# Expert weights in 16 planes, slot rows by one gather, scores and v transposes by halves among the output projection, initial loads in another order

## What is computed

```python
xn = layernorm(x)
q = xn @ Wq + bq                          # 1024 -> 16 heads of 64
k, v = split((xn @ Wdown + bdown) @ Wup + bup)   # through a latent of 256
q, k = rope(q), rope(k)
att = softmax(einsum('thd,tgd->thg', q, k) / 8)  # over the 16 heads g of ONE token
out = einsum('thg,tgd->thd', att, v) @ Wout + bout
logits = xn @ router_w.T + router_b       # 8 experts
y = (xn @ expert_w[top1].T + expert_b[top1]) * max(softmax(logits))
result = x + out + y
```

## Time and profile before

| | us |
|---|---|
| median of three runs | 1162.58 |
| lowest, highest | 1150.81, 1163.72 |
| profiled execution, whole | 1148.63 |
| its span on the slowest core (core 2) | 1147.0 |
| spans of the other cores | 1114.9 to 1141.8 |
| mean granted TensorE clock of core 2 | 0.811 |

### The profile page before, as it was taken

One profiled execution on the slowest core, in us unless ns is written; L12 is line 12 of the kernel. 1 busy time (PEld: TensorE's weight loads), 2 busy tenths in 40 slices (PEclk: granted clock), 3 DMA queues, 4 the chain that ended last, 5 costly groups with the idle time before them and its releaser, 6 DMA issues.

```text
span 1147.0 us, 26610 instructions; the slowest of 8 cores (1114.9 to 1147.0 us)
## 1 busy us (share of the span) xinstructions
PE 768.5 (67%) x10170; PEld 441.5 (38%) x10170; DVE 403.6 (35%) x864; ACT 295.9 (26%) x424; POOL 152.6 (13%) x151
## 2 busy tenths in 40 slices
PE   0626566775857664767866867746362899899984
PEld 0514253544535352545535535433221333333331
DVE  2414434343534443344544534535220121221211
ACT  0313232323241431325234243231220111111110
POOL 2000000000000000000000000001101334344331
PEclk9957676766779686877878878777766999999998
DMA  9966293938577593924335245261932476777785
GB/s 187 191 156 46 95 112 102 151 54 147 41 154 56 158 72 124 142 72 121 78 110 129 38 139 126 52 121 51 189 66 83 93 129 124 135 125 126 129 120 71
DMA packets 73353, 126.64 MB, mean 110 GB/s; under 512 B 12874, under 2 KB 42571, under 8 KB 73236
## 3 DMA queue, kind: packets, MB, share of 16 engines
q0 software_dynamic: 21936, 53.27, 36.5%
q1 hardware_dynamic: 51300, 71.67, 23.8%
HBM read 88.99 MB, written 45.91 MB: 118 GB/s over the span
## 4 chain that ended last, share of the span: by engine, by line
PE 46%; issue 17%; DMA 12%; DVE 9%; SPq 5%; DVEq 5%; ACT 3%; another core or an unknown queue 1%; POOL 0%; ACTq 0%; POOLq 0%
PE ps L1006 17%; PE ps L863 7%; PE ps L814 7%; DMA ks<-ks 6%; PE ps L837 5%; SPq L1022 4%; DMA vs<-vs 4%; DVEq L497 3%; PE ps L948 2%; ACT vs L712 2%; DVE pe L500 2%; DVE stats L399 2%; PE ps L982 2%; PE ps L934 1%; PE ps L902 1%
## 5 line engine op out<-in xcount | busy, mean ns | idle before, releaser
L1006 PE MATMUL ps<-wexp,xgT 128*128 x624 | 200.4, 383 | 22.1 <-issue 20.7
L814 PE MATMUL ps<-wo_sb,oT 128*128 128x512 bf16 x512 | 150.8, 448 | 0.0
L302 POOL DMA_INDIRECT tab<-meta,sloti x32 | 31.5, 985 | 722.9 <-DVEq L471 718.0
L863 PE MATMUL ps<-xnT,wq_sb 128*128 128x256 bf16 x1024 | 121.7, 283 | 0.0
L632 DVE TENSOR_SCALAR y<-ps,metab 128x1024 f32<-128x1024 f32 x39 | 50.1, 1284 | 201.0 <-PE ps L1006 201.0
L1006 PEld LDWEIGHTS ps<-wexp,xgT 128*128 128x128 bf16 x624 | 60.2, 96 | 157.0 <-issue 155.9
L863 PEld LDWEIGHTS ps<-xnT,wq_sb 128*128 128x128 bf16 x1024 | 102.6, 101 | 17.1 <-issue 1.2
L742 ACT COPY xgT<-ps 128x1024 bf16<-128x1024 bf16 x39 | 39.5, 1012 | 227.6 <-PE ps L982 227.6
L837 PE MATMUL ps<-xnT,wdn_sb 128*128 128x256 bf16 x256 | 53.3, 397 | 59.7 <-DVE x1b L512 21.0
L814 PEld LDWEIGHTS ps<-wo_sb,oT 128*128 128x128 bf16 x512 | 57.6, 112 | 80.6 <-issue 47.6
L483 DVE TENSOR_REDUCE mx<-ps 128x16 f32<-128x512 f32 x32 | 21.9, 686 | 165.0 <-PE ps L934 165.0
(11 more groups left out here) (139 smaller groups left out, 823.1 us busy)
## 6 DMA issues: line engine op xcount, KB each, us to landing
xT_sb<-xT SPq DMA_DIRECT2D x16, 1024.0 KB, 8.0
wexp<-exw POOLq DMA_DIRECT2D x16, 1024.0 KB, 22.3
xs<-xn SPq DMA_DIRECT2D x16, 512.0 KB, 9.6
x0b<-x SPq DMA_DIRECT2D x4, 1024.0 KB, 8.2
x1b<-x SPq DMA_DIRECT2D x4, 1024.0 KB
x2b<-x SPq DMA_DIRECT2D x4, 1024.0 KB, 12.2
qs<-qs SPq DMA_DIRECT2D x32, 128.0 KB
ks<-ks SPq DMA_DIRECT2D x32, 128.0 KB
```

Of the source, the lines that this page charges most:

```text
L814: ins = mm(out=ob, lhsT=oT[h][:, 128 * k:128 * k + 128], rhs=wo[:, 1024 * k + 512 * n:1024 * k + 512 * n + 512], start=False, stop=(k == 7))
L863: ins = mm(out=ps[:, 512 * b + 256 * c:512 * b + 256 * c + 256], lhsT=wq[:, 1024 * k + 128 * m:1024 * k + 128 * m + 128], rhs=xnT[:, 256 * ...
L1006: ins = mm(out=bank(2 + 2 * (j % 3) + n), lhsT=xgT[j % 2][:, 128 * k:128 * k + 128], rhs=wexp[:, bass.ds(wof, 8192)] [:, 1024 * k + 512 * ...
```

## The change

**Weights.** The experts' weights become 16 tensors ("planes") `wx[c]`, c = 8n + k, each with one column block of 512 of all eight experts. A matmul's address is the register (512 times the expert) plus its plane's start. Four registers are loaded at a time, once in four tiles. The lower half of each plane (experts 0 to 3, `elo`) is loaded in blocks 1 to 8, two a block, now behind the scatters of the same block; buffers of the first part lie in the upper halves, which are loaded by `ehi` from block 14 on. All weights and the transposed x come from the host in an order in which each partition reads one contiguous piece.

**Table.** `tile_table` moves to block 15 and gives a row number for each tile; one gather brings the 39 rows of 128 slots, and DVE and PE turn them into columns (`meta_rows`, two transposes, `meta_cols`). The first two expert tiles run before the last block's attention and output projection.

**Blocks on PE.** Scores and v transposes run half by half (h outermost), each half in two parts, and parts of the output projection stand between them; its first group stands ahead of `av` of half 1. The banks of the projection and of the latent change. **On DVE** the statistics move a block ahead (those of x(i+2) in block i), `routing2(i)` moves from the end of block i-1 to behind block i's first q evacuation, the projection's evacuations move ahead of `sm2`. **On SP** `xsstore(i+1)` goes first in the loop. **At the start** the first weights are issued before the iotas, `wq` in four pieces with a semaphore each, the five small loads go to ACT's queue.

```diff
+    wx = [at("wx%d" % c, [128, 4096], BF16, EXP0 + 8192 * c) for c in range(16)]
...
+            wload(wdn[:], wdn_d, d_wdn)
+            wload(wq[0][:], wq_d[0], d_wq[0])
             iota(icol[:], [[0, 1]], cm=1)
...
+            def elo(c):
+                wload(wx[c][:, 0:2048], exw_d[c][:, 0:2048], d_elo)
+
+            def ehi(c):
+                wload(wx[c][:, 2048:4096], exw_d[c][:, 2048:4096], d_ehi)
...
-            scatter(0)
             for i in range(NT):
+                scatter(i)
                 if 1 <= i <= 8:
-                    eload((i - 1) // 2, (i - 1) % 2)
-                if i == 14:
+                    elo(2 * i - 2)
+                    elo(2 * i - 1)
+                if i == NT - 2:
                     gpsimd.wait_ge(d_o[0], 32 * 4)
+                    ehi(0)
+                    ehi(1)
                     gpsimd.wait_ge(p_rp, NT)
-                    for half in range(2):
-                        eload(4, half)
-                if i + 1 < NT:
-                    scatter(i + 1)
+                    ehi(2)
+                    ehi(3)
+            gpsimd.wait_ge(p_q, 4 * NT)
+            for c in range(4, 8):
+                ehi(c)
+            gpsimd.wait_ge(p_v, 2 * NT)
+            gpsimd.wait_ge(d_xs, 16 * NT)
+            for c in range(8, 13):
+                ehi(c)
+            gpsimd.wait_ge(d_scat, 32 * NT)
+            gpsimd.wait_ge(v_tab, 1)
+            gpsimd.indirect_dma_start(
+                out=mrow[0:NTILE, :], out_offset=None,
+                in_=re(tab_d, "(t p) two -> t (p two)", p=128),
+                in_offset=bass.IndirectOffsetOnAxis(ap=rowi[0:NTILE, 0:1], axis=0),
+            ).then_inc(d_meta, 16)
+            ehi(15)
             gpsimd.wait_ge(d_o[1], 32 * 4)
...
+            ehi(13)
+            ehi(14)
...
                         proj_evac(b, qs, bq).then_inc(v_q, 1)
-                        if i + 1 < NT and b >= 1 and b < 3:
-                            stats_half(i + 1, b - 1)
-                    if i + 1 < NT:
-                        stats_aggr()
+                        if b == 0:
+                            routing2(i)
...
                     if i + 1 < NT:
                         xnt_evac(i + 1)
+                    else:
+                        tile_table()
+                    if i + 2 < NT:
+                        stats_half(i + 2, 0)
+                        stats_half(i + 2, 1)
+                        stats_aggr()
+                    if i > 0:
+                        op_evac(i - 1, 0, 0)
+                    if i + 1 < NT:
+                        routing1(i + 1)
+                    if i > 0:
+                        op_evac(i - 1, 0, 1)
                     sm1(i, 0)
                     sm1(i, 1)
...
+                    if i > 0:
+                        op_evac(i - 1, 1, 0)
+                    if i == NT - 1:
+                        meta_rows()
+                    if i > 0:
+                        op_evac(i - 1, 1, 1)
+                    if i == NT - 1:
+                        meta_cols()
                     sm2(i, 0)
                     sm2(i, 1)
...
+            def expert_tile(j):
+                if j % 4 == 0:
+                    tensor.reg_load(wreg, tabi[0:1, j:j + 4])
+                tensor.wait_ge(a_gx, j + 1)
+                if j == 4:
+                    tensor.wait_ge(d_ehi, 16 * 16)
+                wof = tensor.snap(wreg[j % 4], min_val=0, max_val=7 * 512)
+                for n in range(2):
+                    for k in range(8):
+                        ins = mm(out=bank(2 * (j % 3) + n),
+                                 lhsT=xgT[j % 2][:, 128 * k:128 * k + 128],
+                                 rhs=wx[8 * n + k][:, bass.ds(wof, 512)],
+                                 start=(k == 0), stop=(k == 7))
+                        release(tensor, [wof * 2 + (EXP0 + 8192 * (8 * n + k))])
...
+                if i >= 2:
+                    tensor.wait_ge(a_avb, i - 1)
+                for m in range(2):
+                    for k in range(8):
+                        ins = mm(out=ps[:, 2560 + 256 * m:2816 + 256 * m],
...
+                    outproj(i - 1, 0, 0, 0, 9)
+                    tensor.wait_ge(a_v, 2 * (i + 1))
...
+                scores(i, 0, 0)
+                if i + 1 < NT:
+                    tensor.wait_ge(a_rp, i + 2)
+                if i > 0:
+                    outproj(i - 1, 0, 1, 0, 4)
+                scores(i, 0, 1)
+                if i > 0:
+                    outproj(i - 1, 0, 1, 4, 9)
+                scores(i, 1, 0)
...
+                if i > 0:
+                    outproj(i - 1, 1, 0, 0, 3)
+                scores(i, 1, 1)
+                if i > 0:
+                    outproj(i - 1, 1, 0, 3, 6)
+                    tensor.wait_ge(v_op, 4 * (i - 1) + 2)
+                tensor.wait_ge(d_xv, 32 * (i + 1))
+                vtrans(i, 0, 0)
+                if i > 0:
+                    outproj(i - 1, 1, 0, 6, 9)
+                vtrans(i, 0, 1)
+                if i > 0:
+                    outproj(i - 1, 1, 1, 0, 4)
+                vtrans(i, 1, 0)
...
+                if i > 0:
+                    outproj(i - 1, 1, 1, 4, 9)
+                vtrans(i, 1, 1)
...
             for i in range(NT + 1):
+                if i + 1 < NT:
+                    xsstore(i + 1)
                 if i >= 2:
                     ostore(i - 2, 1)
                 if i + 2 < NT:
...
-                if i + 1 < NT:
-                    xsstore(i + 1)
-                if i < NT:
                     sync.wait_ge(a_v, 2 * (i + 1))
                     swap(vs, d_xv)
```

More of the change, by code:

```diff
@@ L183, in build_core @@
         d_wdn = sem("d_wdn")
-        d_wq = sem("d_wq")
+        d_wq = [sem("d_wq%d" % b) for b in range(4)]
         d_wk = sem("d_wk")
@@ L207, in build_core @@
         p_op = sem("p_op")
+        p_meta = sem("p_meta")
         p_gx = sem("p_gx")
@@ L349, in _ @@
                 gpsimd.wait_ge(v_y, j + 1)
+                if j == 0:
+                    for b in range(2, 4):
+                        gpsimd.wait_ge(d_o[b], 32 * 4)
                 if j >= 2:
@@ L636, in _ @@
+            for j in range(2, NTILE):
+                y_evac(j)
         @block.scalar
@@ new lines, in scores @@
+            def scores(i, h, part):
+                for o in range(8 * part, 8 * part + 8):
+                    for a in range(4):
+                        tk = 16 * a + o
+                        ins = mm(out=ps[32 * a:32 * a + 32, 512 * h + 32 * o:512 * h + 32 * o + 32],
+                                 lhsT=pair(qs, h, tk), rhs=pair(ks, h, tk),
+                                 start=False, stop=(o == 15), skip_group_check=True,
+                                 tile_position=(64 * h, 32 * a))
+                if part == 1:
+                    ins.then_inc(p_s, 1)
```

694 lines of the change are left out of this document (350 added, 344 removed).

## The result

The changed kernel takes 1055.4 us (median of four runs) against 1163.2 us before. The ratio is 0.910, 95% interval 0.895 to 0.926: faster, by half of what I forecast. I had said 950 us and at most 1050. Ratios compare executions in which neither die of the chip ran slow; the profile of the kernel before is of one in which die 0 was 1.2% longer than die 1, and of a2, b4 and c1 further down the stages are means over the four cores of the undisturbed die.

The account below looks back on a forecast made before the run. Expert tiles were taken as bound by TensorE's address arithmetic, the start by DMA bytes. Tiles -66, blocks -53, -33, -11, start -20, hand-over -24 sum to -207: 942 us against the profiled 1148.6, predicted as 950, range 885 to 1050.

Parts of the forecast that it names:

- slots are scattered from about 9 us on, so the store may land in 3 us; if it meets them, in 12: SP's queue in each block: the x1 store leaves some 6 us in and lands in 3 us, or 12 beside slot scatters.
- span of 33 to 42 us a block: Block length if x lands 22 to 31 us in, with DVE work and v transposes behind it; 38.5 kept for blocks 9 to 13.
- The first rival: Blocks 1 to 14 gain nothing and stay at 53, 45 and 57 us: 1047 us in all; chance 0.17 (nothing or little).
- Its other form, weight loads: Blocks on PE: weight loads of one row half not hidden, about 40 ns a pair, 10 us a block instead of 2.4.
- my 97: Forecast gain of blocks 1 to 14: 53 us in 1 to 8, 33 in 9 to 13, 11 in block 14.
- the sum's 6.7: Net gain a block: 4.0 wdn wait, 2.2 fetches, 1.5 v evacuation, 1.0 clock, less 2.0 us for the halves.
- 2.2 of 4.7: Blocks on PE: of 4.7 us of issue gaps, read as instruction fetches, interleaved projection matmuls hide 2.2.
- the gather lands some 4 us after its issue: Expert tiles: gather time of 3.88 us in the three-buffer loop, one of three limits giving 4.55 us a tile.
- between nothing and 30; I take 20: Start to block 1: DMA bytes bound it, so reordered loads save between nothing and 30 us; 20 taken.
- Forecast -36: Block 15 to tile 0: tile 0 at 60 us instead of 96.3; net -24, as 12 us of projection move among tiles.
- The rival of slow tiles: Expert tiles stay at 5.9 us, one ALU_OP breaking the overlap as three do: 1003 us in all; chance 0.10.
- Both or worse: Blocks gain nothing and tiles stay slow, or worse, to within 2% of the time before; chance 0.05.

Follow-up runs that it names:

- a2: Changed kernel with the swaps of q and k ahead of the store wait and x load on SP's queue: 1057.4 us, ratio 0.909.
- b4: Changed kernel with slot scatters of blocks 0 to 13 behind v's swap, six gather buffers, iotas ahead of the first weight loads: 937.3 us, ratio 0.795.
- c1: Changed kernel with six gather buffers and slots numbered so that 16 following ranks lie 64 bytes apart in the table: 913.6 us, ratio 0.771.
- a4: Changed kernel with six gather buffers instead of three, gathers issued six tiles ahead, slot scatters in place: 1020.0 us, ratio 0.860.
- c3: Changed kernel without slot scatters, with scores and v transposes in quarters of both array halves instead of half by half: 958.3 us, ratio 0.820.
- b3: Kernel before the change without its 32 slot scatters, only blocks read: 1091.1 us, ratio 0.930.
- a3: Changed kernel without its 32 slot scatters, only blocks read: 938.9 us, ratio 0.806.
- c2: Changed kernel with six gather buffers, but the old weight address of three ALU_OPs a matmul: 1078.9 us, ratio 0.924.
- d2: Changed kernel (three gather buffers) without the 39 scatters adding y to the output and their waits, only tiles read: 986.5 us.
- c4: Changed kernel with wo and the biases loaded only once v of block 0 is projected: 1054.1 us from two runs.

## Why the prediction was wrong

**Blocks, 59 us of the 117 missing on this core: the step "slots are scattered from about 9 us on, so the store may land in 3 us; if it meets them, in 12".** Time and place were right (7.9 us in, 8.0 us to landing), the price wasn't. I priced the meeting as a delay of one store, within an unweighted span of 33 to 42 us a block, and kept 38.5. That x lands late and DVE waits for it was named as the new wait and came. But whatever was issued in the next 10 us or so was held: x's load, both swaps (k's issue 6.5 us), and, as I read the 3.78 us of "issue", an instruction fetch. The price was 7.9 us a block in 9 to 13 (5.5 against a4) and 12.0 in 1 to 8 (9.6 against a4), where I took none at all beyond. The earlier trace rows showed a store of 0.5 MB taking 12 us beside two scatters of 1 KB; I read that as sharing, though 2 KB can't share 12 us of 16 engines. The question to ask was what else would lie there after the move. The first rival (1047 us), which I gave 0.17, named this place, and its time is within 1% of the measured one by luck: it lets blocks gain nothing and all else come true, while on the mean of cores blocks 1 to 14 gained 50 us of my 97 and the rest was lost in tiles and start. Its other form, weight loads, is refuted by c3.

**Blocks, what was right, and what only looks so.** The 3.98 us wait before wdn is gone: wdn starts at 534.93 without one. Without slots on either side the gain is 6.2 us a block in 1 to 8 against the sum's 6.7, and 12.0 in 9 to 13. There the clock gave 2 us where I took 1, and the fetches nearly all of their gaps where I took 2.2 of 4.7: PE's waits of b3 before the v transposes (L948) and the scores (L934), 4.8 us a block over all blocks, and behind them the largest of that kind left in a3, 0.8 a block (in all, times, longest, us):

```profile
PE ps L948 <- issue: 51.0, 16, 5.7
PE ps L934 <- issue: 26.4, 11, 4.6
```

```profile
PE ps L891 <- issue: 12.1, 63, 0.3
```

On core 2 of the kernel before, all 28 such gaps of over 1 us ended 1.2 to 1.6 us after a packet of the instruction queue did, which bears out the reading of the earlier trace rows. With the slots in, 9 to 13 gained 5.3 us a block on the mean of cores, near the 6.7: a gain twice the forecast and a cost that I hadn't priced nearly cancel.

**Tiles, 41 us missing: the term "the gather lands some 4 us after its issue".** The 0.31 us for address arithmetic and the 0.22 without it are confirmed from both sides (c2, d2), PE's bound was 3.9. The gather was mis-sized, and not only because the pace rose. Gathers of core 5 in the kernel before, then in the changed one (median us from issue to landing):

```profile
xg<-xs,idxg POOLq DMA_INDIRECT x39, 5.8
```

```profile
xg<-xs,idxg POOLq DMA_INDIRECT x39, 6.6
```

The earlier trace rows showed the first gather, before any y, which nothing disturbed. The old trace already had 5.4 to 5.8 in its loop on the four cores whose landings it holds (4 to 7), beside y's scatters; the faster loop added 0.6 to 0.9, and taking the scatters away gives 3.4 (d2). In the chain of the slowest core they took up to 8.0. Over three buffers 2 to 4 us more are about 1 us a tile, 40 us. Besides, POOL's scatter of y(0) waited 23.3 us for the last store of x, and gather(4) behind it until 838.34, while PE had need of it; the sum has no term for that.

**Start: "between nothing and 30; I take 20".** It was 5 us on the mean of cores. Scatter(0) costs 8 (a3), wo and the biases 5 (c4); the swaps' place on SP's queue gave nothing (a2), POOL's issue order a few us at most (b4). The 20 had no row behind it. In the chain of the changed kernel's start one transfer stands out, k's swap of block 0, behind x(2) and the weights:

```profile
51.00 29.73 DMA ks<-ks
```

The kernel before had 10.64 us for v's swap there. I had named x(2) as wanted in block 0 and given its load no price for the swaps behind it; that the load of x(2) is what they wait for isn't shown, since a2, with the swaps ahead of it, gained nothing.

**Hand-over.** Forecast -36 and found -35.8 on this core, -30.2 on the mean of cores: the row gather was issued 19.4 us into block 15 and landed 27.8 us later, at 47 where I had 45:

```profile
771.84 27.76 DMA mrow<-tab,rowi
```

That it waits for the planes issued ahead of it is in keeping with this, not shown by a run without them. Of the last steps two were off and cancelled: the first gather of a tile was issued 53.1 us into the block, not at 49, and didn't wait long for the three planes ahead of it, since tile 0 began 7.4 us later.

**Block 14** gained 15.3 on this core and 10.4 on the mean for 11. The rival of slow tiles (5.9 us a tile, 1003) came near the tile time, 5.6 us without the 12 us of projection, for a wrong reason: not an ALU_OP but the gather. What came was a good part of both rivals at once. Both or worse I had given 0.05, and my range ended at 1050, inside the first rival's 1000 to 1060, as if the two excluded each other.

## What to carry to other kernels

When an operation moves, ask what it will lie next to, and price it by the worst thing a row shows it doing to a neighbour, not by its own bytes: here 1 KB scatters held megabytes. A transfer's time taken from a quiet row is a lower bound: take it from the middle of the loop, where its company is, and expect more of it when the loop gets faster. One more buffer ahead is cheaper than the estimate. Keep entries that one scatter writes apart from each other, and issue it when nothing urgent comes next.

## What the hardware showed that I had not expected

- 128 writes of 8 bytes to neighbouring entries of DRAM, twice a block, made a block of the changed kernel 7.9 to 12.0 us longer (5.5 to 9.6 by a4's blocks), one of the kernel before 1.2 to 7.4; the same writes 512 bytes apart cost 1.0 to 1.1, and 512-byte rows 0.9. At 64 bytes apart 9 to 13 were free of it, 1 to 8 perhaps not wholly (2.7).
- SP's queue kept the DMA engines 72% busy with 3.07 MB beside the scatters, 55% with 4.46 MB without: they count as busy, as I read it, while a packet is held.
- A scatter that adds 0.5 MB into DRAM makes a 0.25 MB gather beside it land late: medians of 5.4 to 5.8 us in the kernel before and 6.3 to 6.6 in the changed one (cores 4 to 7), 3.4 to 3.5 without the scatters.
- Left open: why cores 0 and 1 of a4 had blocks 1 to 8 at 43 us where the other six had 48 to 50; in another execution of a4 cores 6 and 7 were the short ones (924.9 and 905.6 us against 987 to 1018). Whether a core's scatters also hold other cores' transfers wasn't tried, as all cores run one program.
